# Attention with separate passes for the row maxima: the last head group's four chunks of queries taken in falling order

## The chip, the cores and the metric

One core of a Trainium2 chip. The metric is the device time of one execution in microseconds (us); lower is better.

## What is computed

One transformer block in float32 on x of shape (4, 2048, 256): a layer norm modulated by the condition, causal attention with 16 heads of 16 and rotary embedding, a gated residual, a second modulated layer norm, and a soft mixture of 8 experts. The change touches the attention alone:

```python
q = _rope((h @ Wq.T).reshape(B, S, H, hd).transpose(0, 2, 1, 3))
k = _rope((h @ Wk.T).reshape(B, S, H, hd).transpose(0, 2, 1, 3))
scores = jnp.einsum('bhqd,bhkd->bhqk', q, k) * scale
scores = jnp.where(causal, scores, jnp.finfo(scores.dtype).min)
attn = jax.nn.softmax(scores, axis=-1)
out = jnp.einsum('bhqk,bhkd->bhqd', attn, v)
```

## The kernel before

The four batches run one after the other. In each, the attention stage works through 16 **chunks** k = 0 to 15: four head groups g = k // 4 of 4 heads, and in each four chunks c = k % 4 of 512 queries. Chunk c sees 512(c + 1) keys, so it has 4c + 4 steps of 128 keys (`steps_of_chunk`). A step is cut into **units** of at most 512 columns of scores: 4 units in a full step, 4, 4, 2 and 1 in the four diagonal ones, so 11, 27, 43 and 59 units in the chunks c = 0 to 3, 140 in a head group and SU = 560 in a batch.

For each unit TensorE makes the scores of 128 keys by up to 512 queries in one of three PSUM banks (L634, on a diagonal also the mask, L638), and ScalarE takes the exponential (L913). Three units behind the end of a step, TensorE weighs the values with it (L654, 8 matmuls for 4 heads). After a chunk its result is copied by ScalarE (L902), turned (L664) and divided by its sums on VectorE (L1269, L1271).

The exponential needs the row's maximum beforehand. So there is a second stream, of **maxima**: TensorE makes the same scores with queries on the partitions (L560 to L574) in three other banks, and VectorE reduces each bank (`reduce_unit`, L1188). A chunk c has per head one "diag", one "odd" (two reductions), one "even" and 4c "full" maxima, 4(3 + 4c) = 12, 28, 44 or 60 in all. When a chunk's last one is reduced, VectorE combines them (`negmax`, L1205 to L1214, five small operations). Four maxima into the next chunk stands an entry "rows": TensorE turns the combined maxima (L560), VectorE copies them (L1184), and SP writes them by four DMAs into three extra rows of the queries (`load_bias`, L444). The first score unit of the chunk waits for them. With the 16 "rows" entries a batch has MU = 592 entries in the list MAXES.

The order on TensorE is written out ahead of time: ahead of score unit u it issues maxima until their number is `MAXES_BY[u]`, and VectorE follows the same list. `max_pace` makes it: a linear pace from lead = 60 at u = 0 to all 592 at u = `end`, which is 8 units ahead of the first unit of the last chunk, and at each chunk's first unit at least `ROWS_AT[k] + 8`, so that the chunk's maxima are on the way:

```python
    end = FIRST_UNIT[FIRST_STEP[NK - 1]] - behind
    least = {FIRST_UNIT[FIRST_STEP[k]]: min(MU, ROWS_AT[k] + behind) for k in range(NK)}
        out.append(max(out[-1] if out else 0, min(MU, lead + (MU - lead) * u // end), least.get(u, 0)))
```

The whole list is kept in order: a maximum that is called for early is not called for again, so behind a jump the pace is flat until the line has caught up. The first 41 maxima are made in the stage before (EARLY), 19 more beside the value projections. Keys and queries of a head group come by DMAs issued by ScalarE at fixed units (L916 to L922), and the output projection starts when all 16 chunks are done (L709).

Of the kernel before, what the change touches and what calls it, by code (L numbers as in the profile page):

```python
# [11 lines left out]
NC = 4  # L12
# [22 lines left out]
NG = H // HG  # L35
NK = NG * NC
VC = HD + 1


def steps_of_chunk(k):  # L40

    return 4 * (k % NC) + 4


STEPS = [(k, j) for k in range(NK) for j in range(steps_of_chunk(k))]
# [5 lines left out]
def diagonal(s):  # L51

    k, j = STEPS[s]
    return max(j - 4 * (k % NC), -1)

# [9 lines left out]

def max_units_of_chunk(k):

    c = k % NC  # L70
    for h in range(HG):
        yield k, h, "diag", 0, 0
        yield k, h, "odd", 0, 0
        yield k, h, "even", 0, 0
        for kc in range(c):
            for r in range(4):
                yield k, h, "full", r, kc
# [80 lines left out]
def adaln_block(nc, x, Wq, Wk, Wv, Wo, norm_gamma, slot_gamma, slot_embeds, w1, b1, w2, b2, cond, wmod,  # L158
                rope_cos, rope_sin, ident_in, mask_in, maskT_in, out):
    f32, bf16 = mybir.dt.float32, mybir.dt.bfloat16  # L160
    ALU, ACT, AX = mybir.AluOpType, mybir.ActivationFunctionType, mybir.AxisListType
# [8 lines left out]
    with ctx:  # L170
# [216 lines left out]
        def _(sp):  # L387
# [49 lines left out]
            for b in range(B):  # L437

                def load_bias(k):

                    g, c = divmod(k, NC)
                    sp.wait_ge(s_mxf, b * MU + (ROWS_AT[k] + 1 + NMX))
                    for h in range(HG):
                        sp.dma_start(qst[g % 2][KROWS:BROWS, h, c * CH:(c + 1) * CH],  # L444
                                     nrow[4 * PARTS * h:4 * PARTS * (h + 1), k % 3, :]).then_inc(s_bias[k % 3], 16)

                for k in range(NK):
                    load_bias(k)
                    if k == 0:
                        sp.wait_ge(s_o, b * NT) if b else None  # L450
                        sp.dma_start(modb[:, :, :].rearrange("p n d -> p (n d)"), mod_park[b:b + 1, :].to_broadcast([P, 4 * D])
                                     ).then_inc(s_modl, 16)
                sp.wait_ge(s_st, b * SU + (LAST_UNIT_OF_CHUNK[3 * NC - 1] + 1))
                sp.dma_start(xres, x[b].rearrange("(t p) d -> p t d", p=P)).then_inc(s_xr, 16)

                for c in range(NC):
                    sp.wait_ge(s_x1, b * 8 + 2 * c + 2)
                    sp.dma_start(x1_park[b, :, 1024 * c:1024 * c + 1024],
                                 xres[:, 4 * c:4 * c + 4, :].rearrange("p t d -> p (t d)")).then_inc(s_park, 16)

                def load_expert(e):
                    sp.dma_start(w1s[e % NR], w1[e].rearrange("(k p) h -> p k h", p=P)).then_inc(s_ew[e % NR], 16)
                    sp.dma_start(w2s[e % NR], w2[e].rearrange("(j p) d -> p j d", p=P)).then_inc(s_ew[e % NR], 16)
                for e in range(NR):
                    sp.wait_ge(s_sl, b * 16 + 4 * (e + 1))
                    load_expert(e)
                sp.wait_ge(s_sl, b * 16 + 16)
                sp.dma_start(b2b, b2.rearrange("(o e) d -> o e d", o=1).to_broadcast([P, E, D])).then_inc(s_b2, 16)
                if b + 1 < B:
                    load_x(b + 1)  # L470
                for e in range(NR, E):
                    sp.wait_ge(s_y, b * 8 + e - NR + 1)
                    load_expert(e)
                sp.wait_ge(s_eo, b * 8 + 8)
                sp.wait_ge(s_park, (b + 1) * 64)
                for c in range(NC):
                    sp.dma_start(x1[:, 4 * c:4 * c + 4, :].rearrange("p t d -> p (t d)"),
                                 x1_park[b, :, 1024 * c:1024 * c + 1024]).then_inc(s_x1r[c], 16)
                if b + 1 < B:
                    qkv_transfers(b + 1)  # L480
# [4 lines left out]
        def _(pe):  # L485
# [52 lines left out]
            def max_unit(b, m):  # L538

                k, h, kind, r, kc = MAXES[m]  # L540
                g, c = divmod(k, NC)
                bank = NST + m % NMX
                if m == FIRST_MAX[k]:
                    if g == 0:
                        if c == 0:
                            pe.wait_ge(s_rab, (b + 1) * QU)
                            pe.wait_ge(s_id, 1)
                        pe.wait_ge(s_ldf[c], (b + 1) * 112)
                    elif c == 0:
                        pe.wait_ge(s_ld[g % 2], (b * LOAD_USES[g % 2] + (g + 1) // 2) * 112)  # L550
                pe.wait_ge(s_mxf, b * MU + (m + 1))

                def qt(i):
                    return qst[g % 2][0:KROWS, h, i * P:(i + 1) * P]

                def kt(i, n):
                    return kst[g % 2][0:KROWS, h, i * P:(i + n) * P]
                if kind == "rows":
                    pe.wait_ge(s_nm, b * NK + (k + 1))
                    last = tr(ps[0:PARTS * HG * 4, bank, 0:P // 2].bitcast(bf16),  # L560
                              negp[:, :, :, :].rearrange("p h s t -> p (h s t)"), identb[:, :])
                elif kind == "diag":
                    mm(ps[:, bank, :], identb[:, :], maskb[:, :, :].rearrange("p r t -> p (r t)"),  # L563
                       start=True, stop=True)
                    for i in range(4):
                        last = mm(ps[:, bank, i * P:(i + 1) * P], qt(4 * c + i), kt(4 * c + i, 1),
                                  start=False, stop=True, skip_group_check=True)
                elif kind == "odd":
                    mm(ps[:, bank, 0:P], qt(4 * c + 1), kt(4 * c, 1), start=True, stop=True)
                    last = mm(ps[:, bank, P:4 * P], qt(4 * c + 3), kt(4 * c, 3), start=True, stop=True)  # L570
                elif kind == "even":
                    last = mm(ps[:, bank, 0:2 * P], qt(4 * c + 2), kt(4 * c, 2), start=True, stop=True)
                else:
                    last = mm(ps[:, bank, :], qt(4 * c + r), kt(4 * kc, 4), start=True, stop=True)  # L574
                last.then_inc(s_mx, 1)
# [29 lines left out]
            for b in range(B):  # L605
# [17 lines left out]
                def score_unit(u):  # L623

                    s, h0, n, w = UNITS[u]
                    k, j = STEPS[s]
                    g, c = divmod(k, NC)
                    if s == FIRST_STEP[k] and u == FIRST_UNIT[s]:
                        pe.wait_ge(s_bias[k % 3], (b * BIAS_USES[k % 3] + k // 3 + 1) * 64)
                    if u >= NST:  # L630
                        pe.wait_ge(s_ex, b * SU + (u + 1 - NST))
                    bank = ps[:, u % NST, :]
                    for i in range(n):
                        last = mm(bank[:, i * w:(i + 1) * w], kst[g % 2][0:BROWS, h0 + i, j * P:(j + 1) * P],  # L634
                                  qst[g % 2][0:BROWS, h0 + i, (c + 1) * CH - w:(c + 1) * CH],
                                  start=i == 0, stop=True, skip_group_check=True)
                    if diagonal(s) >= 0:
                        last = mm(bank[:, 0:n * w].rearrange("p (n w) -> p n w", n=n)[:, :, 0:P], identb[:, :],  # L638
                                  maskTb[:, 0:n, :], start=False, stop=True, skip_group_check=True)
                    last.then_inc(s_st, 1)  # L640

                def weigh(s):

                    k, j = STEPS[s]
                    g, c = divmod(k, NC)
                    w = CH - max(diagonal(s), 0) * P
                    if j == 0:
                        if k:
                            pe.wait_ge(s_ev, b * NK + k)
                        else:  # L650
                            pe.wait_ge(s_vone, b + 1)
                    pe.wait_ge(s_ex, b * SU + (LAST_UNIT[s] + 1))
                    for h in range(HG):
                        last = mm(ps[32 * h:32 * h + VC, 6, CH - w:CH], vall[:, j, HG * g + h, :], Eb[s % ESLOTS][:, h, 0:w],  # L654
                                  start=j == 0, stop=True, skip_group_check=True)
                    last.then_inc(s_pvq, 1)
# [449 lines left out]
        def _(dve):  # L1106
# [95 lines left out]
            def negmax(b, k):  # L1202

                dve.wait_ge(s_mxf, b * MU + (LAST_MAX[k] + 1 + NMX))
                V.tensor_reduce(negm[:, :, :], pm[:, k % 2, :, :, 0:2 + k % NC], AX.X, ALU.max, negate=True).then_inc(s_own_nm, 1)  # L1205
                at = 4 * (b * NK + k)
                dve.wait_ge(s_own_nm, at + 1)
                V.tensor_copy(negp[:, :, 0, :], negm[:, :, :]).then_inc(s_own_nm, 1)
# [50 lines left out]
            for b in range(B):  # L1259

                def gather(k):

                    g, c = divmod(k, NC)
                    if k == 0:
                        for i in range(QU - SETS_OF_BATCH[b], QU):
                            dve.wait_ge(s_pk[set_of(b, i)], set_parked(b, i))
# [190 lines left out]
```

## Time and profile before

| | us |
|---|---|
| median of 3 runs | 3474.62 (3473.63 to 3474.74) |
| the profiled execution | 3468.5, its span 3466.7 |
| TensorE busy | 3148.6 (91%) |
| VectorE busy | 2254.7 (65%) |
| ScalarE busy | 1848.3 (53%) |
| attention stage of one batch (first to last exponential) | 454.3 to 455.9, four times |

Times in the trace count from the start of the span. The k-th exponential of L913 in a batch is unit k, so the trace shows when each unit passes. Batch 1 runs its units from 1001.2 to 1456.7 us. A busy TensorE is not TensorE at its peak: the ends of its matmuls are modelled.

### The profile page before, as it was taken

The numbers are of one execution on the slowest core, as the hardware profiler recorded it, in microseconds if no ns is written. First come the engines' busy times: TensorE is split into PE (matmuls) and PEld (weight loads), VectorE is DVE, ScalarE is ACT, GpSimd is POOL, SyncE is SP. The second block draws the span as 40 slices with busy tenths as digits, with TensorE's granted clock in tenths as the row PEclk, the third lists the DMA queues.
The fourth block names the chain that finished last, engine by engine and source line by source line (L and its number), as shares of the span: only waits on it lengthen the run. The fifth ranks groups of instructions, "written<-read, shape, count | busy, mean of one in ns | idle before, by whom it ended". The sixth has DMA issues, their size and how long they took to land.

```text
span 3466.7 us, 45370 instructions
## 1 busy us (share of the span) xinstructions
PE 3148.6 (91%) x17663; PEld 1541.5 (44%) x17663; DVE 2254.7 (65%) x4309; ACT 1848.3 (53%) x3425; POOL 253.1 (7%) x139
## 2 busy tenths in 40 slices
PE   5799999898899999888989999988997999998999
PEld 2433332547553333353754333334575333333468
DVE  5878884662677788366367788836536877874632
ACT  2366667464236666645515666655641566665560
POOL 3100000110400000011030000000122000001100
PEclk9799999999999999999999999999999999999999
DMA  5222200015412120002542202010353221101042
GB/s 147 71 38 38 38 2 26 25 60 181 137 38 35 23 38 2 31 19 96 169 118 50 38 2 38 1 43 7 128 169 98 38 39 22 18 10 41 0 159 97
DMA packets 123694, 202.01 MB, mean 58 GB/s; under 512 B 10108, under 2 KB 107136, under 8 KB 120372
## 3 DMA queue, kind: packets, MB, share of 16 engines
q1 hardware_dynamic: 110960, 148.71, 13.3%
q10 hardware_dynamic: 12520, 50.40, 7.7%
q8 instruction: 140, 2.29, 0.3%
q14 instruction: 74, 0.61, 0.1%
HBM read 156.14 MB, written 42.16 MB: 57 GB/s over the span
## 4 chain that ended last, share of the span: by engine, by line
PE 71%; DVE 12%; ACT 7%; DMA 3%; issue 3%; POOL 2%; ACTq 1%; SPq 1%; DVEq 0%
PE ps L654 15%; PE ps L634 11%; PE ps L574 9%; PE ps L778 7%; PE ps L587 6%; DVE pm L1188 5%; PE ps L752 5%; ACT R L913 2%; PE ps L794 2%; DMA R<-in_L_ffn_w_dram 2%; PE ps L534 2%; PE ps L804 2%; PE ps L619 1%; PE ps L741 1%; PE ps L638 1%
## 5 line engine op out<-in xcount | busy, mean ns | idle before, releaser
L1188 DVE TENSOR_REDUCE pm<-ps 128x1 f32<-128x512 f32 (+4 forms) x2560 | 1395.2, 603 | 265.9 <-PE ps L574 190.1
L913 ACT ACTIVATE R<-ps 128x512 f32<-128x512 f32 (+1 forms) x2240 | 1190.5, 588 | 612.1 <-PE ps L634 418.7
L634 PE MATMUL ps<-R 99*128 99x512 bf16 (+3 forms) x2560 | 822.7, 354 | 26.8 <-ACT R L913 16.0
L654 PE MATMUL ps<-R 128*17 128x512 f32 (+3 forms) x5120 | 598.9, 541 | 24.5 <-ACT R L902 24.0
L574 PE MATMUL ps<-R 96*128 96x512 bf16 x1536 | 575.2, 385 | 24.7 <-DVE pm L1188 21.7
L634 PEld LDWEIGHTS ps<-R 99*128 99x128 bf16 x2560 | 238.4, 98 | 249.7 <-ACT R L913 139.6
L574 PEld LDWEIGHTS ps<-R 96*128 96x128 bf16 x1536 | 147.3, 97 | 453.1 <-DVE pm L1188 346.2
L778 PE MATMUL ps<-R 128*128 128x512 f32 x512 | 233.6, 615 | 12.2 <-ACT R L1005 12.2
L587 PE MATMUL ps<-R 128*128 128x257 f32 x1024 | 235.3, 385 | 4.1 <-ACT R L861 3.6
L752 PE MATMUL ps<-snT,R 128*128 128x512 f32 x512 | 229.8, 594 | 6.3 <-ACT R L951 6.3
L587 PEld LDWEIGHTS ps<-R 128*128 128x128 f32 x1024 | 196.5, 193 | 41.2 <-issue 12.1
L654 PEld LDWEIGHTS ps<-R 128*17 128x17 f32 x5120 | 86.1, 96 | 240.4 <-ACT R L913 117.9
L1096 POOL TENSOR_TENSOR R<-R,modb 128x1024 f32<-128x1024 f32 x16 | 37.6, 2349 | 2099.7 <-DVE R L1307 2099.7
L638 PE MATMUL ps<-maskTb,identb 128*128 128x128 bf16 (+2 forms) x704 | 172.6, 245 | 0.0
L778 PEld LDWEIGHTS ps<-R 128*128 128x128 f32 x512 | 100.6, 198 | 145.9 <-issue 124.8
L1269 DVE RECIPROCAL rden<-ps 128x16 f32<-128x16 f32 x64 | 16.0, 250 | 228.8 <-PE ps L664 228.8
L794 PE MATMUL ps<-R 128*128 128x128 f32 x1024 | 130.6, 291 | 27.9 <-DMA R<-in_L_ffn_w_dram 15.1
L563 PE MATMUL ps<-maskb,identb 128*128 128x512 bf16 x256 | 102.9, 402 | 56.9 <-DVE pm L1188 31.5
L1379 DVE TENSOR_TENSOR R<-ps,R 128x256 f32<-128x256 f32 x32 | 13.6, 425 | 204.7 <-PE ps L804 204.7
L794 PEld LDWEIGHTS ps<-R 128*128 128x128 f32 x1024 | 126.8, 205 | 37.4 <-DMA R<-in_L_ffn_w_dram 20.5
L894 ACT COPY R<-ps 128x512 f32<-128x512 f32 x32 | 18.7, 585 | 230.3 <-PE ps L619 230.3
L752 PEld LDWEIGHTS ps<-snT,R 128*128 128x128 f32 x512 | 93.0, 190 | 106.1 <-issue 95.6
(154 smaller groups left out, 3357.9 us busy)
## 6 DMA issues: line engine op xcount, KB each, us to landing
R<-in_L_ffn_w_dram SPq DMA_DIRECT2D x64, 1024.0 KB, 7.0
R<-q_parts ACTq DMA_DIRECT2D x12, 768.0 KB
R<-k_parts ACTq DMA_DIRECT2D x12, 768.0 KB
R<-in_L_attn_x_dram SPq DMA_DIRECT2D x16, 512.0 KB, 8.1
q_parts<-R SPq DMA_DIRECT2D x16, 512.0 KB, 3.8
k_parts<-R SPq DMA_DIRECT2D x16, 512.0 KB, 3.4
R<-in_L_attn_x_dram SPq DMA_DIRECT2D x4, 2048.0 KB, 8.4
x_park<-R SPq DMA_DIRECT2D x16, 512.0 KB, 2.6
```

Of the source, the lines that this page charges most:

```text
L534: last = mm(ps[:, 2 + 2 * qk + f, :], wqkT[:, k, 2 * qk + f, :], hT[:, k, c * CH:(c + 1) * CH], start=k == 0, stop=k == 1)
L563: mm(ps[:, bank, :], identb[:, :], maskb[:, :, :].rearrange("p r t -> p (r t)"), start=True, stop=True)
L574: last = mm(ps[:, bank, :], qt(4 * c + r), kt(4 * kc, 4), start=True, stop=True)
L587: last = mm(ps[:, 6 + n % 2, 0:D + 1], EcT[:, e, n * P:(n + 1) * P], eo[:, e, :], start=e == 0, stop=e == E - 1)
L634: last = mm(bank[:, i * w:(i + 1) * w], kst[g % 2][0:BROWS, h0 + i, j * P:(j + 1) * P], qst[g % 2][0:BROWS, h0 + i, (c + 1) * CH - w:(c + ...
L638: last = mm(bank[:, 0:n * w].rearrange("p (n w) -> p n w", n=n)[:, :, 0:P], identb[:, :], maskTb[:, 0:n, :], start=False, stop=True, skip_ ...
L654: last = mm(ps[32 * h:32 * h + VC, 6, CH - w:CH], vall[:, j, HG * g + h, :], Eb[s % ESLOTS][:, h, 0:w], start=j == 0, stop=True, skip_grou ...
L752: last = mm(ps[:, 4 + 2 * (n % 2) + mh, :], xnT[:, k, n * P:(n + 1) * P], snT[:, k, mh * 512:(mh + 1) * 512], start=k == 0, stop=k == 1)
L778: last = mm(ps[:, 2 * k + mh, :], xn[:, n, k * P:(k + 1) * P], L[:, n, mh * 512:(mh + 1) * 512], start=n == 0, stop=n == NT - 1)
L794: last = mm(ps[:, 2 * (e % 2) + j // 4, (j % 4) * P:(j % 4 + 1) * P], w1s[e % NR][:, k, j * P:(j + 1) * P], slotsT[:, k, e * P:(e + 1) * P ...
L913: A(Eb[s % ESLOTS][:, h0:h0 + n, 0:w], ps[:, u % NST, 0:n * w].rearrange("p (n w) -> p n w", n=n), ACT.Exp, scale=SCALE).then_inc(s_ex, 1)
L1188: mx = lambda o, i: V.tensor_reduce(o, i, AX.X, ALU.max)
```

## The change

`group_and_chunk(k)` takes the place of `divmod(k, NC)` and `k % NC` where a chunk's place is needed: in head group 3 the chunks k = 12 to 15 now stand for c = 3, 2, 1, 0 in place of 0, 1, 2, 3. All else follows from that: the order of units and maxima, the due times, and through FIRST_UNIT of chunk 15 the slope of the pace. The number of instructions on each engine is the same.

```diff
--- before.py
+++ after.py
@@ -37,9 +37,15 @@
 VC = HD + 1
 
 
+def group_and_chunk(k):
+
+    g, c = divmod(k, NC)
+    return g, NC - 1 - c if g == NG - 1 else c
+
+
 def steps_of_chunk(k):
 
-    return 4 * (k % NC) + 4
+    return 4 * group_and_chunk(k)[1] + 4
 
 
 STEPS = [(k, j) for k in range(NK) for j in range(steps_of_chunk(k))]
@@ -51,7 +57,7 @@
 def diagonal(s):
 
     k, j = STEPS[s]
-    return max(j - 4 * (k % NC), -1)
+    return max(j - 4 * group_and_chunk(k)[1], -1)
 
 
 
@@ -67,7 +73,7 @@
 
 def max_units_of_chunk(k):
 
-    c = k % NC
+    c = group_and_chunk(k)[1]
     for h in range(HG):
         yield k, h, "diag", 0, 0
         yield k, h, "odd", 0, 0
@@ -438,7 +444,7 @@
 
                 def load_bias(k):
 
-                    g, c = divmod(k, NC)
+                    g, c = group_and_chunk(k)
                     sp.wait_ge(s_mxf, b * MU + (ROWS_AT[k] + 1 + NMX))
                     for h in range(HG):
                         sp.dma_start(qst[g % 2][KROWS:BROWS, h, c * CH:(c + 1) * CH],
@@ -538,7 +544,7 @@
             def max_unit(b, m):
 
                 k, h, kind, r, kc = MAXES[m]
-                g, c = divmod(k, NC)
+                g, c = group_and_chunk(k)
                 bank = NST + m % NMX
                 if m == FIRST_MAX[k]:
                     if g == 0:
@@ -546,7 +552,7 @@
                             pe.wait_ge(s_rab, (b + 1) * QU)
                             pe.wait_ge(s_id, 1)
                         pe.wait_ge(s_ldf[c], (b + 1) * 112)
-                    elif c == 0:
+                    elif k % NC == 0:
                         pe.wait_ge(s_ld[g % 2], (b * LOAD_USES[g % 2] + (g + 1) // 2) * 112)
                 pe.wait_ge(s_mxf, b * MU + (m + 1))
 
@@ -624,7 +630,7 @@
 
                     s, h0, n, w = UNITS[u]
                     k, j = STEPS[s]
-                    g, c = divmod(k, NC)
+                    g, c = group_and_chunk(k)
                     if s == FIRST_STEP[k] and u == FIRST_UNIT[s]:
                         pe.wait_ge(s_bias[k % 3], (b * BIAS_USES[k % 3] + k // 3 + 1) * 64)
                     if u >= NST:
@@ -642,7 +648,7 @@
                 def weigh(s):
 
                     k, j = STEPS[s]
-                    g, c = divmod(k, NC)
+                    g, c = group_and_chunk(k)
                     w = CH - max(diagonal(s), 0) * P
                     if j == 0:
                         if k:
@@ -1202,7 +1208,7 @@
             def negmax(b, k):
 
                 dve.wait_ge(s_mxf, b * MU + (LAST_MAX[k] + 1 + NMX))
-                V.tensor_reduce(negm[:, :, :], pm[:, k % 2, :, :, 0:2 + k % NC], AX.X, ALU.max, negate=True).then_inc(s_own_nm, 1)
+                V.tensor_reduce(negm[:, :, :], pm[:, k % 2, :, :, 0:2 + group_and_chunk(k)[1]], AX.X, ALU.max, negate=True).then_inc(s_own_nm, 1)
                 at = 4 * (b * NK + k)
                 dve.wait_ge(s_own_nm, at + 1)
                 V.tensor_copy(negp[:, :, 0, :], negm[:, :, :]).then_inc(s_own_nm, 1)
@@ -1260,7 +1266,7 @@
 
                 def gather(k):
 
-                    g, c = divmod(k, NC)
+                    g, c = group_and_chunk(k)
                     if k == 0:
                         for i in range(QU - SETS_OF_BATCH[b], QU):
                             dve.wait_ge(s_pk[set_of(b, i)], set_parked(b, i))
```

## Rows read from the trace of the kernel before

**Rows 1.** The page: span, busy time of the engines, costliest groups of the attention stage

```profile
span 3466.7 us, 45370 instructions
...
PE 3148.6 (91%) x17663; PEld 1541.5 (44%) x17663; DVE 2254.7 (65%) x4309; ACT 1848.3 (53%) x3425; POOL 253.1 (7%) x139
...
L1188 DVE TENSOR_REDUCE pm<-ps 128x1 f32<-128x512 f32 (+4 forms) x2560 | 1395.2, 603 | 265.9 <-PE ps L574 190.1
L913 ACT ACTIVATE R<-ps 128x512 f32<-128x512 f32 (+1 forms) x2240 | 1190.5, 588 | 612.1 <-PE ps L634 418.7
L634 PE MATMUL ps<-R 99*128 99x512 bf16 (+3 forms) x2560 | 822.7, 354 | 26.8 <-ACT R L913 16.0
L654 PE MATMUL ps<-R 128*17 128x512 f32 (+3 forms) x5120 | 598.9, 541 | 24.5 <-ACT R L902 24.0
L574 PE MATMUL ps<-R 96*128 96x512 bf16 x1536 | 575.2, 385 | 24.7 <-DVE pm L1188 21.7
```

**Rows 2.** Windows over the attention stage of batch 1 and of batch 0; columns as named

```profile
core 0: us, PE busy (x) PEld busy (x) DVE busy (x) ACT busy (x) POOL busy (x), PEclk, DMA share, GB/s
1001.00:1457.00 456.00, 435.51 (x2939) 153.79 (x2940) 336.59 (x687) 302.80 (x576) 0.00 (x0) 0.98 0.15 27
150.00:606.00 456.00, 434.29 (x2936) 153.58 (x2935) 336.68 (x687) 302.21 (x575) 0.00 (x0) 0.98 0.15 27
```

**Rows 3.** Windows of batch 1: full pace with maxima, and the tail without maxima

```profile
1315.00:1355.00 40.00, 39.77 (x267) 14.46 (x267) 33.46 (x70) 27.48 (x52) 0.00 (x0) 1.00 0.01 2
1426.00:1450.00 24.00, 21.68 (x128) 4.87 (x124) 0.68 (x2) 20.75 (x41) 0.00 (x0) 1.00 0.07 23
```

**Rows 4.** Windows, exponentials (L913) alone: the same two stretches

```profile
core 0: us, ACT busy (x), PEclk, DMA share, GB/s
1315.00:1355.00 40.00, 27.48 (x52) 1.00 0.01 2
1426.00:1450.00 24.00, 20.75 (x41) 1.00 0.07 23
```

**Rows 5.** Groups kept apart by form: the reductions of the maxima (mean ns of one)

```profile
L1188 DVE TENSOR_REDUCE pm<-ps 128x1 f32<-128x512 f32 x1536 | 972.9, 683 | 192.1 <-PE ps L574 190.1
L1188 DVE TENSOR_REDUCE pm<-ps 128x4 f32<-128x512 f32 x256 | 175.5, 686 | 30.2 <-PE ps L566 27.8
L1188 DVE TENSOR_REDUCE pm<-ps 128x1 f32<-128x384 f32 x256 | 139.7, 546 | 0.0
L1188 DVE TENSOR_REDUCE pm<-ps 128x1 f32<-128x256 f32 x256 | 106.1, 415 | 22.9 <-PE ps L572 21.0
...
L1188 DVE TENSOR_REDUCE pm<-ps 128x1 f32<-128x128 f32 x256 | 72.1, 282 | 20.6 <-PE ps L570 20.3
```

**Rows 6.** Timeline of DVE in the burst ahead of unit 81, batch 1; start, length, what

```profile
1065.15 0.69 DVE L1188 TENSOR_REDUCE pm<-ps 128x1 f32<-128x512 f32 x1 [0.59 <-PE ps L574]
1065.87 0.23 DVE L1205 TENSOR_REDUCE negm<-pm 128x16 f32<-128x80 f32 x1
...
1066.77 0.17 DVE L1214 TENSOR_TENSOR negp<-negr,negp 128x16 bf16<-128x16 f32 x1
1066.86 2.42 DVE L1188 TENSOR_REDUCE pm<-ps 128x4 f32<-128x512 f32 x5
1069.20 0.21 DVE L1184 COPY nrow<-ps 48x128 bf16<-48x128 bf16 x1
1069.36 1.09 DVE L1188 TENSOR_REDUCE pm<-ps 128x1 f32<-128x128 f32 x3
1070.62 3.17 DVE L1188 TENSOR_REDUCE pm<-ps 128x4 f32<-128x512 f32 x7 [0.17 <-PE ps L566]
```

**Rows 7.** Timeline of ACT at the three bursts of batch 1

```profile
1062.90 1.81 ACT L913 ACTIVATE R<-ps 128x512 f32<-128x512 f32 x3
1074.18 1.08 ACT L913 ACTIVATE R<-ps 128x512 f32<-128x512 f32 x2 [9.47 <-PE ps L634]
...
1184.06 1.32 ACT L913 ACTIVATE R<-ps 128x512 f32<-128x512 f32 x2
1191.97 1.08 ACT L913 ACTIVATE R<-ps 128x512 f32<-128x512 f32 x2 [6.60 <-PE ps L634]
...
1306.60 0.60 ACT L913 ACTIVATE R<-ps 128x512 f32<-128x512 f32 x1 [0.17 <-PE ps L638]
1311.04 1.09 ACT L913 ACTIVATE R<-ps 128x512 f32<-128x512 f32 x2 [3.84 <-PE ps L634]
```

**Rows 8.** Windows: the bursts ahead of units 81 and 221, and maxima alone in the prologue

```profile
1064.70:1074.00 9.30, 6.95 (x39) 3.20 (x35) 8.12 (x22) 0.01 (x1) 0.00 (x0) 0.66 0.01 1
1185.00:1191.90 6.90, 4.80 (x35) 1.83 (x27) 6.07 (x16) 0.38 (x1) 0.00 (x0) 0.91 0.01 2
110.00:120.00 10.00, 9.33 (x28) 2.94 (x28) 10.00 (x23) 0.00 (x0) 0.00 (x0) 0.50 0.23 69
```

**Rows 9.** One line (L634), all of it: the score matmuls, ns min/median/max

```profile
L634 PE MATMUL ps<-R x2560: 216/379/635, 149.3 to 3152.3; 99*128 99x512 bf16 x139, 99*128 99x384 bf16 x20, 99*128 99x128 bf16 x19, 99*128 99x256 bf16 x19
```

**Rows 10.** Windows, exponentials (L913) alone: 9 us behind the burst at unit 221, batches 1 and 2

```profile
1191.90:1200.90 9.00, 4.97 (x9) 0.50 0.01 2
2042.60:2051.60 9.00, 7.03 (x14) 1.00 0.00 0
```

**Rows 11.** Timeline of SP in the burst at unit 81: the rows of maxima to the queries

```profile
1069.43 2.92 SPq L444 DMA_DIRECT2D R<-nrow  x4
```

**Rows 12.** Timeline: end of the attention stage of batch 1

```profile
1455.73 1.57 ACT L913 ACTIVATE R<-ps 128x512 f32<-128x512 f32 x3
...
1456.43 1.49 PE L654 MATMUL ps<-R 128*17 128x384 f32 x24
...
1457.99 0.58 ACT L902 COPY R<-ps 128x512 f32<-128x512 f32 x1 [0.68 <-PE ps L654]
...
1459.61 0.42 DVE L1271 TENSOR_TENSOR R<-ps,rden 128x256 f32<-128x256 f32 x1
...
1460.09 1.09 PE L705 MATMUL ps<-ident,R 128*128 128x128 f32 x8 [0.81 <-DVE R L1271]
```

## The prediction

> **What bounds the kernel now.** I began with the page: TensorE is busy for 91% of the span, VectorE 65%, ScalarE 53%, and three of the five costliest groups are TensorE's matmuls of the attention stage [rows 1]. The windows over that stage show it four times alike, 456 us, TensorE busy for 434 to 436 of them [rows 2]. So attention takes 4 x 455 = 1820 of the 3467 us, and there TensorE is the engine to watch.
>
> The change leaves the work alone and alters its order, so I need prices for the three ways in which the plan mixes the two streams:
> - **Mixed**, at the full pace of (592 - 60) / 493 = 1.079 maxima per score unit. In 40 us 52 exponentials pass, 0.769 us per unit [rows 4], with TensorE busy 39.77 of 40 us and VectorE 33.46 [rows 3]. TensorE bounds it.
> - **Flat**, score units without maxima, as in the tail of a batch: 41 exponentials in 24 us, 0.585 us per unit [rows 4]; TensorE is busy 21.68 us, ScalarE 20.75, VectorE nearly idle [rows 3]. The pair and its three banks bound it.
> - **Burst**, maxima without score units, where a due time lifts the plan. Before batch 1's unit 81 there are 13, before 221 there are 10, before 361 there are 7. ScalarE idles there for 9.47, 6.60 and 3.84 us [rows 7], and VectorE is at work almost throughout [rows 6, 8]. A burst runs at VectorE's price: 683 ns for a full one, 686 a diagonal one, 282 + 546 an odd one, 415 an even one [rows 5], 0.21 for "rows" and 1.1 for the five operations of a chunk's end [rows 6]. For the 13: 4 x 0.686 + 4 x 0.828 + 3 x 0.415 + 0.683 + 0.21 + 1.1 = 9.3 us; exponential to exponential was 1074.18 - 1064.11 = 10.07 [rows 7] (the three from 1062.90 on end at 1064.71, and the last began 0.60 earlier), less about 0.54 for the score unit itself, 9.5. The price holds.
>
> **What the change does to the plan.** I worked out MAXES_BY from the formula for both orders.
>
> The slope's end moves from unit 493 to 560 - 11 - 8 = 541, as chunk 15 now has 11 units. The pace falls from 1.079 to 532 / 541 = 0.983. The due times don't fall with it. At unit 420 (chunk 12) the maxima of a chunk with c = 3 are now wanted, 60 and not 12: due are ROWS_AT + 8 = 516, the pace has brought 472 at unit 419, and 44 come at once; before, only 468 were due and the pace was at 513. At 479 chunk 13 wants 561 where 530 are there, 31; at 522 chunk 14 wants 590, 18 more. In head groups 0 to 2, whose order is unchanged, the slower pace makes the old jumps larger and opens new ones: 21 at unit 81 (13 before), 12 at 178, 31 at 221 (10), 4 at 291, 23 at 318, 41 at 361 (7). Behind every jump the plan is flat until the line has caught up.
>
> Per batch: maxima in bursts 30 before, 225 after (+195). Units in flat stretches 90 before (66 of them the tail from 494 on), 239 after (+149).
>
> **The sum.** Let p be what a unit costs TensorE-bound, q what a maximum adds to it; p + 1.079 q = 0.769. Units and maxima are the same in number, so only what leaves the mix changes the time:
> change = 149 (0.585 - p) + (burst time after - before) - 195 q.
> - Burst time after: 144 full, 24 diagonal, 26 odd, 23 even and 8 "rows" make 98.4 + 16.5 + 21.5 + 9.5 + 1.7 = 147.6 us, and 7 chunk ends 7.7: 155.3. Before, by the same prices, 18.9 + 1.1 = 20.0. Difference 135.3 us.
> - q: no row shows it alone. The shortest score matmul, as wide as a full maximum, is 216 ns [rows 9]; I take 0.216, so p = 0.536. If the flat stretch were TensorE-bound too, q = (0.769 - 0.585) / 1.079 = 0.170 at least; the mean duration of a full maximum, with its pipeline, is 0.385 at most [rows 1]. The sum hardly depends on it: 0.170 gives 0 + 135.3 - 33.2 = 102.1; 0.216 gives 7.3 + 135.3 - 42.1 = 100.5; 0.385 gives 149 x 0.231 = 34.4, so 34.4 + 135.3 - 75.1 = 94.6. I take **100.5 us per batch**.
> - TensorE's clock. In a burst TensorE waits for VectorE (4.80 us busy of 6.90), and in the first two bursts of batch 1 the granted clock falls to half (means 0.66 and 0.91) [rows 8]. It stays there into the flat stretch: in the 9 us behind unit 221 batch 1 passes 9 exponentials at 0.50, batch 2, where it did not fall, 14 at 1.00 [rows 10]. That is 1.0 us against 0.64 per unit, 3.2 us. After the change eight bursts per batch have 12 maxima or more. At 3 us each that is 24; before, one full and one partial such loss, about 4. I add **20 us per batch**. Bounds: nothing (the clock comes back inside a long burst) and 43.
> - The burst itself costs no more at half clock: in the prologue VectorE is busy 10.0 of 10.0 us with maxima at 0.50 [rows 8].
> - "Rows": SP issues four DMAs in 2.92 us from 1069.43 [rows 11], and the exponential comes at 1074.18 [rows 7], 0.4 us behind the last maximum (1070.62 + 3.17). The eight entries from "rows" on cover the DMAs, as they will in every burst. Nothing; if SP were late, 1 us for each of eight.
> - The order itself: head group 3's keys come before chunk 8 begins and serve all four chunks, and the output projection waits for all of them. The last chunk ends in the same four diagonal steps, so the drain of some 4 us [rows 12] stays. Nothing; at most 1 us either way.
>
> 120.5 x 4 = 482 us. The profiled execution, 3468.5 us, would become 3950; the median lies 6.1 above it, so **3956**, taken as 3955.
>
> The rule for the clock is also in the Trainium skill (TensorE: Matmul & The Clock Gate, "Part 1: The HAM clock gate"): half rate is the array's default state, and activity releases it. It speaks against every long burst; without it the sum would be 3877, with it 3956.
>
> **The rivals.**
> - **The clock comes back only with the mix** (7%). All 239 flat units then run at 1.0 us, 0.415 more each, 99 us in place of 24: 195 per batch, 3474.6 + 782 = 4257. For it: 9 us at 0.50 behind a burst [rows 10]. Against it: TensorE is busy for most of a flat stretch, and the batch 1 tail runs at 1.00 throughout [rows 3].
> - **No more is lost to the clock than before** (15%): 3474.6 + 4 x 100.5 = 3877. For it: behind unit 221 of batch 2 nothing was lost [rows 10].
> - **Faster** (2%): the due times at 420, 479 and 522 don't decide, and what counts is the shorter tail. The flat stretches would shrink from 90 to 24 + 18 units with bursts as before: -48 x 0.049 = -2.4 us per batch, 3465; with q = 0.385, -48 x 0.231 = -11, 3430. It needs the pace to lie above 516 at unit 420; it is at 473. Above that point nothing bursts in group 3.
> - **No effect** (1%): the jumps are absorbed, as ScalarE has slack. It would need more than three score banks between the engines, since ScalarE stopped for 9.47 us at 13 maxima [rows 7].
>
> The forecast itself has 75%.
>
> **How the numbers follow.** Low end: 94 per batch and no clock loss, 3474.6 + 376 = 3851. High end: 102 per batch and a clock loss of 43 more than before, 3474.6 + 580 = 4055. With the rival at 4257 left out and misses of the price of a burst allowed for (0.1 us per burst maximum would be 78 us), about 2 in 10 lie outside 3850 to 4060. 0.2% is what a measurement of this kernel can tell from no change, 7 us; every case but two is far beyond it: slower 0.97, same 0.01, faster 0.02.
>
> **What would show it.** Attention per batch 575 us and not 455, and the other stages the same. VectorE's and ScalarE's busy time unchanged, TensorE's share near 80%. Idle of ScalarE ahead of unit 420 of some 29 us, 28 at 361, 20 at 221 and 479, each released by a score matmul, with VectorE busy through it. Flat stretches behind them at 0.59 us per unit, 1.0 for the first few where the clock is at half. Mixed stretches at 0.536 + 0.983 x 0.216 = 0.75. Wrong would be: bursts that run faster than 0.6 us per maximum, or an idle ScalarE that falls short of these lengths; a second wait on the "rows" DMAs; half clock through whole flat stretches.

## The result, and the profile after

The changed kernel takes 3950.4 us (median; 3948.2 to 3956.2) against 3474.1 us: a ratio of 1.137, 95% interval 1.1355 to 1.1384. The forecast was 3955. It was right in size and in mechanism, but several of its terms were off and cancelled.

From the page of the changed kernel: span, busy time, two slice rows, and the groups that answer to [rows 1]. The line numbers are 6 higher than before.

```profile
span 3954.4 us, 45207 instructions
...
PE 3438.9 (87%) x17500; PEld 1588.8 (40%) x17663; DVE 2254.4 (57%) x4309; ACT 1831.7 (46%) x3425; POOL 253.3 (6%) x139
...
PEclk9888878899998887899999887789999988788999
DMA  5320100115422010011532110000242212000033
...
L1194 DVE TENSOR_REDUCE pm<-ps 128x1 f32<-128x512 f32 (+4 forms) x2560 | 1388.7, 603 | 668.2 <-PE ps L580 350.9
L919 ACT ACTIVATE R<-ps 128x512 f32<-128x512 f32 (+1 forms) x2240 | 1173.5, 588 | 1113.0 <-PE ps L640 943.5
L640 PE MATMUL ps<-R 99*128 99x512 bf16 (+3 forms) x2560 | 832.0, 380 | 139.1 <-DMA R<-nrow 96.6
L580 PE MATMUL ps<-R 96*128 96x512 bf16 x1536 | 643.5, 438 | 81.3 <-DVE pm L1194 76.5
```

VectorE's and ScalarE's busy times have hardly moved. What grew is idle time: VectorE ahead of its reductions from 265.9 to 668.2 us, ScalarE ahead of its exponentials from 612.1 to 1113.0 us, 500 us more. Each engine waits for TensorE while TensorE works through the entries of the other stream. TensorE's own busy time rose by 290 us without an added instruction, and its mean granted clock fell from 0.965 to 0.883: it ran at half clock for longer. And one releaser is new among the large ones: `DMA R<-nrow`, the rows of maxima, 96.6 us.

Windows of batch 1 of the changed kernel: the whole attention stage, the burst ahead of unit 420, and two stretches of the flat plan behind it. They answer to [rows 2, 3, 8].

```profile
core 0: us, PE busy (x) PEld busy (x) DVE busy (x) ACT busy (x) POOL busy (x), PEclk, DMA share, GB/s
1121.00:1697.00 576.00, 505.93 (x2898) 164.29 (x2936) 335.88 (x687) 298.26 (x575) 0.00 (x0) 0.84 0.12 21
1541.00:1567.00 26.00, 21.79 (x57) 5.53 (x56) 25.83 (x52) 0.00 (x0) 0.00 (x0) 0.59 0.00 1
1568.00:1576.40 8.40, 8.04 (x37) 2.25 (x37) 0.41 (x2) 4.84 (x9) 0.00 (x0) 0.50 0.01 2
1576.40:1583.60 7.20, 6.56 (x37) 1.22 (x35) 0.27 (x1) 6.22 (x13) 0.00 (x0) 0.99 0.00 1
```

The stage takes 576 us where it took 456. In the burst VectorE is busy 25.83 of 26 us and ScalarE does nothing. Behind it the clock is at 0.50 for 8.4 us, then at 0.99.

Timeline of ScalarE in the same batch, at unit 151, then ahead of units 361 and 420, answering to [rows 7]:

```profile
1257.45 0.60 ACT L919 ACTIVATE R<-ps 128x512 f32<-128x512 f32 x1 [7.58 <-PE ps L640]
...
1473.29 0.60 ACT L919 ACTIVATE R<-ps 128x512 f32<-128x512 f32 x1 [0.35 <-PE ps L644]
1499.56 1.09 ACT L919 ACTIVATE R<-ps 128x512 f32<-128x512 f32 x2 [25.67 <-PE ps L640]
...
1568.01 1.09 ACT L919 ACTIVATE R<-ps 128x512 f32<-128x512 f32 x2 [27.46 <-PE ps L640]
```

The two long stops stand where the plan has its jumps of 41 and 44. The first one, at unit 151, stands where the plan has no jump at all.

### The profile page after: what moved, and what is told of

The parts are those of the page before. It is cut to its first block, busy times and chain, and to the rows that moved or that the text cites. A ratio compares the mean times of both kernels' runs of the same rounds, so it can differ in the third digit from the quotient of the medians.

```text
span 3954.4 us, 45207 instructions
## 1 busy us (share of the span) xinstructions
PE 3438.9 (87%) x17500; PEld 1588.8 (40%) x17663; DVE 2254.4 (57%) x4309; ACT 1831.7 (46%) x3425; POOL 253.3 (6%) x139
## 3 DMA queue, kind: packets, MB, share of 16 engines
q1 hardware_dynamic: 110960, 148.71, 11.8%
## 4 chain that ended last, share of the span: by engine, by line
PE 61%; DVE 18%; ACT 7%; DMA 7%; issue 3%; SPq 2%; POOL 1%; ACTq 1%; DVEq 0%
PE ps L660 14%; PE ps L640 12%; DVE pm L1194 11%; PE ps L784 5%; PE ps L593 5%; PE ps L580 5%; DMA R<-nrow 4%; PE ps L758 4%; ACT R L919 3%; PE ps L800 2%; DMA R<-in_L_ffn_w_dram 2%; PE ps L540 2%; PE ps L810 2%; SPq L450 2%; PE ps L625 1%
## 5 line engine op out<-in xcount | busy, mean ns | idle before, releaser
L1194 DVE TENSOR_REDUCE pm<-ps 128x1 f32<-128x512 f32 (+4 forms) x2560 | 1388.7, 603 | 668.2 <-PE ps L580 350.9
L919 ACT ACTIVATE R<-ps 128x512 f32<-128x512 f32 (+1 forms) x2240 | 1173.5, 588 | 1113.0 <-PE ps L640 943.5
L640 PE MATMUL ps<-R 99*128 99x512 bf16 (+3 forms) x2560 | 832.0, 380 | 139.1 <-DMA R<-nrow 96.6
L580 PE MATMUL ps<-R 96*128 96x512 bf16 x1536 | 643.5, 438 | 81.3 <-DVE pm L1194 76.5
L660 PE MATMUL ps<-R 128*17 128x512 f32 (+3 forms) x5120 | 637.0, 574 | 27.6 <-ACT R L908 21.3
L572 PE MATMUL ps<-R 96*128 96x128 bf16 x1024 | 119.7, 249 | 44.6 <-DVE maskTb L1250 14.9
L644 PE MATMUL ps<-maskTb,identb 128*128 128x128 bf16 (+2 forms) x665 | 156.8, 236 | 0.0
```

What stands on the lines that cost most here:

```text
L919: A(Eb[s % ESLOTS][:, h0:h0 + n, 0:w], ps[:, u % NST, 0:n * w].rearrange("p (n w) -> p n w", n=n), ACT.Exp, scale=SCALE).then_inc(s_ex, 1)
L1194: mx = lambda o, i: V.tensor_reduce(o, i, AX.X, ALU.max)
```

## The account of one batch

The start times of the 560 exponentials of batch 1, sorted by what the plan does ahead of each unit, give this account (us; the change as forecast stands beside it):

| | before | after | change | forecast |
|---|---|---|---|---|
| units with a burst ahead (3; 9) | 21.7 | 162.1 | +140.4 | 135.3 + 6 x 0.536 = +138.5 |
| flat units (90; 239) | 59.6 | 169.5 | +109.9 | 149 x 0.585 + 20 = +107.2 |
| mixed units (466; 311) | 374.3 | 244.2 | -130.1 | -155 x 0.536 - 195 x 0.216 = -125.2 |
| sum | 455.6 | 575.8 | +120.2 | +120.5 |

The first row counts the gap from the exponential before the burst to the one behind it. In the first row are 10.7 us, and in the third 7.4 us, of a wait that the forecast had at nothing. The gap at unit 291 lasts 14.3 us for 4 maxima worth 2.7 by the forecast's prices and 0.8 for the unit itself; that at unit 151 lasts 8.2 us where 0.8 is usual in the mix. Without these waits the bursts cost 129.7 and not 138.5, and the mix saves 137.5 and not 125.2.

## Experiments

All ratios are against the kernel before, on the same chip.

**1. Order and slope apart.** The falling order with the old slope:

```diff
+++ changed kernel, max_pace
-    end = FIRST_UNIT[FIRST_STEP[NK - 1]] - behind
+    end = 493
```

> The falling order kept, the slope of the pace put back by hand (end = 493 in place of 541). Theory (the lost time comes from the flatter slope alone): 34 maxima in bursts and 93 flat units per batch, as before but for one jump of 4 at unit 420, so 1 us per batch: 3474 + 4 = 3478 us, 3465 to 3490. Rival (the order itself costs, since the chunk with most keys now comes first in its group and wants 60 maxima at once): the three bursts of group 3, 93 of the 195 added burst maxima, stay, and some 40% of the loss with them: about 3665 us.

Measured: 3485.5 us, ratio 1.0027 (1.0015 to 1.004). And the rising order with the new slope:

```diff
+++ kernel before, max_pace
-    end = FIRST_UNIT[FIRST_STEP[NK - 1]] - behind
+    end = 541
```

> The rising order of before, with the flatter slope alone (end = 541). Theory (slope alone): 221 maxima in bursts, 234 flat units, eight bursts over 12: by the same prices 118 us per batch, 3948 us, 3920 to 3975. Rival (order and slope each bring their part): bursts of groups 0 to 2 only, 132 maxima, 102 more than before, about 62 us per batch: 3722 us.

Measured: 3959.7 us, ratio 1.139 (1.137 to 1.1405). So the slope alone brings the whole loss, in either order, and the order alone 10 us of 476. The rising kernel now has its own long stop ahead of its last chunk, 41 maxima at unit 501. Timeline of ScalarE in it:

```profile
1633.35 2.31 ACT L913 ACTIVATE R<-ps 128x384 f32<-128x384 f32 x4 [1.04 <-PE ps L638]
1666.31 1.08 ACT L913 ACTIVATE R<-ps 128x512 f32<-128x512 f32 x2 [30.65 <-PE ps L634]
```

The diff does not touch the line that did it. `end` hangs on the length of the last chunk: 59 units at the end kept the pace steep, 11 units don't. The steep line was behind the due time at 3 of the 15 later chunks; the flat one is behind at 9 of them, and what is missing is then made up at once.

The order by itself costs 10 us where 4 were expected. In the trace of the steep falling kernel chunk 11, with the jump of 4 behind it, takes 1.6 to 3.5 us longer per batch than before. In two of the four batches the clock also falls to half behind unit 361, where the plan is still that of before, so not all of the 10 us need be the order's. The steep falling kernel there, then the kernel before at the same place in batch 1:

```profile
1315.90:1322.70 6.80, 6.60 (x32) 1.24 (x32) 2.04 (x4) 4.24 (x8) 0.00 (x0) 0.50 0.00 0
1310.20:1317.00 6.80, 5.95 (x48) 2.21 (x47) 3.50 (x12) 4.78 (x9) 0.00 (x0) 1.00 0.01 2
```

**2. The clock behind a burst.** Needless matmuls behind each maximum of the eight long bursts, into the bank of the output transposes. The added wait lets TensorE write there only when VectorE has read what an earlier chunk left in it:

```diff
+                    burst = u and MAXES_BY[u] - MAXES_BY[u - 1] > 10
+                    if burst:
+                        pe.wait_ge(s_on, b * NK + STEPS[UNITS[u][0]][0] - 1)
                     while m < MAXES_BY[u]:
                         max_unit(b, m)
                         m += 1
+                        if burst:
+                            for w in (512, 256):
+                                mm(ps[:, 7, 0:w], zerosb[:, :], maskb[:, :, :].rearrange("p r t -> p (r t)")[:, 0:w],
+                                   start=True, stop=True)
```

> The changed kernel, with two needless matmuls of 512 and 256 columns into the bank of the output transposes behind each maximum of the eight long bursts, so that TensorE is busy in them. They add work and nothing to the output. Theory (3.0 us behind six bursts and 1.3 behind two are the clock at half, and it falls since TensorE waits in the burst): the granted clock stays at 1.00 from burst to flat, the bursts keep their length (0.22 + 0.32 us of TensorE under 0.62 of VectorE), and 4 x 20.6 = 82 us go: 3868 us, 3850 to 3895. Rival (the slow units behind a burst are the start of the pipeline and three banks, whatever the clock): no change or slower, 3950 to 3990.

Measured: 3849.8 us, ratio 1.108 (1.106 to 1.110), so 101 us less than the changed kernel for more work. Below are windows of the burst ahead of batch 1's unit 420 and of the 5.4 us behind it, then ScalarE's stop there in the timeline.

```profile
1494.00:1520.00 26.00, 24.85 (x144) 12.37 (x145) 25.52 (x51) 0.00 (x0) 0.00 (x0) 1.00 0.01 1
1521.10:1526.50 5.40, 4.57 (x37) 1.48 (x36) 0.14 (x1) 4.77 (x9) 0.00 (x0) 1.00 0.00 0
```

```profile
1521.19 2.30 ACT L926 ACTIVATE R<-ps 128x512 f32<-128x512 f32 x4 [27.34 <-PE ps L640]
```

The clock is at 1.00 in both, where it was 0.59 and 0.50. The stop has its old length, 27.34 us for 27.46, so the burst goes at VectorE's pace at either clock level. The first 8 units behind each of the eight bursts take 5.44 or 5.45 us in this batch, where the changed kernel takes 8.43 (six times) and 6.73 or 6.74 (twice). The half clock, and not the start of the pipeline, is what makes these units dear. That is 20.6 us per batch, 82 in all, of the 101 gained. By the start times of all four batches, the flat units as a whole take 89 us less than in the changed kernel, the units with a burst 11 us less (0.1 to 0.5 us for each gap), the mixed ones 3. The time at half clock within the four attention stages falls from 734 to 82 us; before it was 68.

The Trainium skill (TensorE: Matmul & The Clock Gate, "Part 1: The HAM clock gate") says that activity releases the half rate, and this pair of runs agrees: the same burst with TensorE kept at work shows 1.00, against 0.59.

**3. The two stops without a burst.** Timelines of the changed kernel, batch 1: ScalarE issues the queries and keys of group 3 behind unit 279; SP issues chunk 9's rows of maxima; then come the last three exponentials ahead of the stop, and that of unit 291.

```profile
1380.99 1.26 ACTq L386 DMA_DIRECT2D R<-q_parts  x3
1382.28 1.81 ACTq L388 DMA_DIRECT2D R<-k_parts  x4
...
1388.74 2.92 SPq L450 DMA_DIRECT2D R<-nrow  x4
...
1389.81 1.81 ACT L919 ACTIVATE R<-ps 128x512 f32<-128x512 f32 x3 [0.56 <-PE ps L644]
1405.28 1.09 ACT L919 ACTIVATE R<-ps 128x512 f32<-128x512 f32 x2 [13.67 <-PE ps L640]
```

The rows go out at 1388.7, and the exponential that needs them starts at 1405.3. In the burst of the kernel before, they were issued at 1069.43 [rows 11] and used at 1074.18 [rows 7]. The DMA queues of the changed kernel show what is under way in between. Queue q10 carries ScalarE's seven transfers, 3.1 MB in all, and q1 the four of SP, 3 KB each. The first line is the window 1388 to 1397 us, in which q1 has no packet; the other two are 1397 to 1403.5 us:

```profile
q10 hardware_dynamic: 135, 1.49, 100.4%
q10 hardware_dynamic: 79, 0.66, 53.5%
q1 hardware_dynamic: 60, 0.01, 1.6%
```

The last packet of the rows starts 14.5 us behind the issue, where it was 3.7 us in the burst at unit 81 before. At unit 151 it is 18.0 us, though SP issues the rows there 1.0 us ahead of ScalarE's first transfer. I moved the large transfers:

```diff
-                        if u == LAST_UNIT_OF_CHUNK[NC * (g - 1) - 1]:
+                        if u == LAST_UNIT_OF_CHUNK[NC * (g - 1) - 1] + 13:
                             load_group(act, g, slice(0, T), s_ld[g % 2])
```

> The changed kernel, with the keys and queries of head groups 2 and 3 fetched 13 units later (behind the first units of chunks 5 and 9, not ahead of them). In the changed kernel's trace ScalarE waits 14.3 us ahead of unit 291, where only 4 maxima stand, and 8.2 us ahead of unit 151, where there is no burst; the rows of maxima were issued just behind the 1.5 MB of keys there. Theory (the small transfers queue behind the large ones): both waits go, 10.7 + 7.4 = 18 us per batch, 3950 - 72 = 3878 us, 3860 to 3900. Rival (SP or the maxima are late by themselves there): no change, 3950.

Measured: 3862.1 us, ratio 1.111 (1.109 to 1.113): 88 us less than the changed kernel. The gap from unit 290 to 291 falls from 14.3 to 2.5 us, that from 150 to 151 from 8.2 to 1.3. SP and ScalarE at unit 291 of that run:

```profile
1359.11 2.92 SPq L450 DMA_DIRECT2D R<-nrow  x4
1363.87 0.60 ACT L919 ACTIVATE R<-ps 128x512 f32<-128x512 f32 x1 [1.89 <-PE ps L640]
```

So the large transfers had held up the small ones. By this the two waits are 11.8 and 6.9 us per batch, 75 in all. In the kernel before, the steeper pace had sent chunk 5's rows off at 1107.3 us in batch 1, and the large transfers followed at 1117.4.

That is 16 us more than the 72 expected. I put them down to ScalarE's own issue, and tested that in the kernel before, with the same edit:

> The kernel before, with the keys of head groups 2 and 3 fetched 13 units later and nothing else. Theory (late keys brought 88 us in the changed kernel: 72 by the two waits for rows of maxima, which the kernel before does not have, and 16 by ScalarE's issue of the DMAs at the chunk's end, which it has): 3475 - 16 = 3459 us. Rival (all of the 88 us are waits for rows of maxima): 3475.

Measured: 3495.2 us, ratio 1.0053 (1.0033 to 1.0073). Both expectations fail: it is 20 us slower. ScalarE in batch 1 of that run:

```profile
1140.34 0.60 ACT L913 ACTIVATE R<-ps 128x512 f32<-128x512 f32 x1 [0.22 <-PE ps L634]
1140.35 1.41 ACTq L380 DMA_DIRECT2D R<-q_parts  x3
1141.79 1.79 ACTq L382 DMA_DIRECT2D R<-k_parts  x4
1143.63 1.57 ACT L913 ACTIVATE R<-ps 128x512 f32<-128x512 f32 x3 [2.69 <-issue]
```

The seven issues stop ScalarE for 2.69 us in the midst of the mix, where TensorE soon waits for it. The stops at units 140 and 280 did shorten, from 3.2 to 1.6 and from 3.4 to 1.4 us in batch 1, but chunk 5 then took 27.2 us in place of 23.7. The clock has a part in that: behind each of the eight such stops of this run it is at half for 3.4 us, and at none of these places in the kernel before. How much of the price that is was not set apart. Behind unit 151 of batch 1, first this run, then the kernel before:

```profile
1146.10:1149.50 3.40, 3.40 (x16) 1.37 (x9) 0.69 (x1) 1.17 (x3) 0.00 (x0) 0.51 0.97 142
1135.40:1138.80 3.40, 3.40 (x23) 1.15 (x22) 3.37 (x7) 2.17 (x4) 0.00 (x0) 1.00 0.47 87
```

The start times of the changed kernel with late keys place its gain in batch 1, 20.6 us: 18.7 are the two waits, 4.1 the shorter stops at units 140 and 280, and 1.7 the units behind the burst at 318, which pass sooner at full clock. The moved issues take some 3 us of that back in chunks 4, 5 and 8. Why they take 8.6 us back in the kernel before (chunks 4, 5, 8 and 9) is open.

**4. The pace levelled.** If a maximum costs more in a burst than in the mix, a plan without bursts must beat both kernels. Between the due times it takes the smallest slopes that meet them all:

```diff
+    points = [(0, values_by(7))] + [(FIRST_UNIT[FIRST_STEP[k]], min(MU, ROWS_AT[k] + behind)) for k in range(1, NK)]
+    out = [0] * SU
+    at = points[0]
+    while at[1] < MU:
+        to = max((p for p in points if p[0] > at[0] and p[1] > at[1]),
+                 key=lambda p: ((p[1] - at[1]) / (p[0] - at[0]), p[0]))
+        for u in range(at[0], to[0] + 1):
+            out[u] = at[1] - (-(to[1] - at[1]) * (u - at[0]) // (to[0] - at[0]))
+        at = to
+    for u in range(at[0], SU):
+        out[u] = MU
```

> The falling order, with the pace levelled: between the due times it takes the smallest slopes that meet them all (1.22, 1.06, 1.03, 0.76, 0.67 maxima per unit), so there is no burst at all, 35 flat units. Theory (a burst maximum costs 0.65 us where one in the mix costs 0.22 to 0.3, and a flat unit saves almost nothing): 20 us per batch less than before, 3394 us, 3375 to 3430. Rival (the mix is bound at 0.77 us per unit by VectorE's pace, so that 1.22 per unit stalls as a burst does): 3474 or more.

> The rising order with the same levelling of the pace: slopes 1.22, 1.06, 0.98, all maxima made by unit 501, no burst, 59 flat units at the end. Theory: 19 us per batch less than before, 3398 us, 3380 to 3435, so within 0.5% of the falling order with the levelled pace: the order is then worth the spread of 24 flat units, under 2 us per batch. Rival (the falling order is worth something by itself once the plan is level, since its tail is shorter): the falling one faster by over 20 us.

Measured: falling 3391.6 us, ratio 0.9756 (0.974 to 0.977); rising 3432.2 us, 0.988 (0.986 to 0.990). The falling one came out as expected and is the fastest kernel of this study. Its attention stage, and in it a stretch with the steepest pace and one with the gentlest:

```profile
981.00:1416.00 435.00, 423.61 (x2932) 151.37 (x2934) 337.54 (x687) 303.92 (x574) 0.00 (x0) 1.00 0.15 28
1010.00:1045.00 35.00, 33.85 (x224) 11.52 (x223) 31.46 (x61) 22.80 (x43) 0.00 (x0) 1.00 0.56 92
1365.00:1405.00 40.00, 38.60 (x277) 13.60 (x275) 19.55 (x49) 32.09 (x62) 0.00 (x0) 1.00 0.01 3
```

435 us at a clock of 1.00, TensorE 97% busy over the stage, VectorE at 90% where the pace is steep. The rising one lies at the upper end of its range, and its rival held: the order is worth 40 us here, not under 8. Part of it is a wait ahead of unit 501, where the last due time leaves nothing to cover the rows of maxima. Waits of the rising levelled kernel around it (us in total, times, longest):

```profile
ACT R L918 <- PE ps L639: 5.1, 3, 3.8
PEld ps L639 <- DMA R<-nrow: 3.8, 1, 3.8
PE ps L639 <- DMA R<-nrow: 3.1, 1, 3.1
```

So I had all maxima made by unit 493, with one more point:

```diff
+    points.append((493, MU))
```

> The rising order with the levelled pace and all maxima due by unit 493 in place of 501, as the pace of before had it. Theory (of the 9 us per batch that the rising levelled kernel takes above the falling one, 3.4 are the wait for the last rows of maxima at unit 501, whose DMAs nothing covers): 3432 - 4 x 3 = 3420 us, 3412 to 3428; the rest of the gap to 3392 stays. Rival (all of the gap is that wait): 3395. Second rival (the wait moves to 493 with its cost): 3432.

Measured: 3406.5 us, ratio 0.980 (0.9785 to 0.982). It gained 26 us, twice the forecast. The forecast counted the wait alone, and the clock goes with it. In and behind unit 501's wait the rising levelled kernel is at half clock for 6.8 us, and with the early end it is not. Windows of batch 1, first without and then with the early end:

```profile
1395.60:1402.40 6.80, 4.00 (x22) 0.82 (x22) 0.00 (x0) 1.99 (x4) 0.00 (x0) 0.50 0.58 181
1384.50:1391.30 6.80, 5.83 (x51) 1.85 (x44) 0.00 (x0) 5.70 (x13) 0.00 (x0) 1.00 0.59 187
```

15 us remain between the orders. The rising order makes its last maxima within the 81 units of three short chunks and leaves 59 flat units, or 66 with the early end; the falling order spreads them up to unit 536. In the traces head group 3 takes 98.1 us of batch 1 in the rising order with the early end and 94.9 in the falling one, so most of the 4 us per batch lie there. That these units are the cause was not tested.

Last, the levelled falling plan with the late keys:

> The falling order with the levelled pace and the keys of head groups 2 and 3 fetched 13 units later. Theory (issuing the seven DMAs costs ScalarE 3.1 us while it holds up the exponentials at units 140 and 280, where it waits 3.2 to 4.5 us; behind the first units of a chunk this is hidden): 2 x 2.2 us per batch, 3392 - 18 = 3374 us. Rival (the stop at 140 and 280 is the end of the chunk, and comes with any order of issue): 3392, or above it if the later keys collide with other rows of maxima.

Measured: 3410.5 us, ratio 0.981 (0.979 to 0.983), 19 us slower than without them. The edit helped only where rows of maxima were held up; in a level plan none are, and the stop in the mix is all that it brings, as in the rising kernel (20 us). Here too the clock has a part: the time at half clock within the four attention stages rises from 3 to 34 us.

## Why the prediction was right, and where it was not

- **The plan.** Bursts of 21, 12, 31, 4, 23, 41, 44, 31 and 18 maxima were worked out from the formula, and ScalarE stops there. That the slope's end moves with the last chunk was the decisive reading, and experiment 1 confirms it. The prediction gave due times and slope the credit together; the runs give it to the slope: with the steep one the due time at 420 asks for 4 more maxima and not 44.
- **The price of a burst.** Summing the mean durations of the reductions gave 152.5 us for the eight bursts other than 291; they take 143.5 (gaps less 0.54 for the unit). At unit 420 the sum says 29.2 + 1.1 = 30.3 us, and the gap, score unit included, is 28.06. Reductions back to back start closer than they last. In this burst 12 full ones, recorded at 0.678 us each, fill 7.3 us with no idle time, where 12 x 0.678 would be 8.1; their starts lie 0.60 us apart. The reductions that run between 1544.4 and 1550.9 us:

```profile
L1194 DVE TENSOR_REDUCE pm<-ps 128x1 f32<-128x512 f32 x12 | 7.3, 678 | 0.0
```

The forecast's test of the price, the burst at unit 81, came out right by luck. The overlap is there as well (the diagonal one that starts at 1066.86 lasts 0.686 us, and the next starts 0.60 behind it), but VectorE was busy for only 8.12 of 9.30 us [rows 8], and its idle time made up for what the sum had too much.
- **What the mix gives back.** -137.5 us and not -125.2. The forecast's bounds (94.6 to 102.1 in the sum) took one p for every unit. At these prices the 466 mixed units of before should take 358 us; they take 374. The units at a chunk's start are dearer than the rest: in batch 1 of the kernel before, mixed units among the first 12 of a chunk take 0.87 us, the others 0.77. The 168 units that leave the mixed class took 6.5 us more than their price, and with a burst ahead of them they now pass in the flat class. Another 6.0 us come from 298 units that are mixed in both kernels and became cheaper by more than q for each maximum that left them. Why these did is open; no run set either part apart.
- **The 0.216.** It was read off the wrong row. The shortest score matmul is not as wide as a full maximum: it is the form of 128 columns, and one of 512 columns is recorded at 388 ns in the mean. The value is right all the same, since the 512-column matmuls of the maxima (L574) start 0.217 us apart at the median in the trace before. That was luck, and by the forecast's own bounds the sum hardly hung on it. From the kernel before:

```profile
L634 PE MATMUL ps<-R 99*128 99x512 bf16 x1792 | 666.2, 388 | 24.8 <-ACT R L913 14.0 <-DMA R<-nrow 8.9
L634 PE MATMUL ps<-R 99*128 99x128 bf16 x256 | 25.1, 220 | 0.0
```

- **The rows of maxima.** "Nothing; if SP were late, 1 us for each of eight" was the step that failed: two waits, 7.4 and 10.7 us, 72 us over four batches. I had looked at bursts only. The slower pace also makes the rows later where there is no burst, and twice a batch that put them among 3.1 MB of queries and keys (the expectation of late_keys names 1.5 MB, the keys alone). A second wait on the "rows" DMAs was among the prediction's own signs of being wrong, and it came.
- **The clock.** 20 us per batch were added. Experiment 2 finds 3.0 us behind six bursts and 1.3 behind two, 20.6 us. The kernel before had 4.3 of it in batch 1 (6.74 and 8.43 us for 8 units where 5.44 is full clock), so the net is 16.3 and not 20. (The upper bound of 43 stands in the prediction without a working.) The flat units made up for it: their row is 2.7 us above the forecast, so apart from the clock they cost 6.4 us more than 149 x 0.585. With the clock held up they take 0.618 us each (147.8 us for 239). Of the rivals, "no more is lost to the clock" falls, and so does "the clock comes back only with the mix": it is back 8.4 us into the flat stretch.
- **Faster, or no effect.** Neither: the due times did bite, and of the 28.06 us at unit 420 ScalarE idles for 27.46, so the three score banks absorb next to nothing.
- **The signs.** Stage and stops came as named (576 us for 575; 27.5, 25.7 and about 20 us). TensorE's share did not: near 80% was named, and it is 87% of the span and 88% of the stage, as its matmuls last longer at half clock (those of the maxima 438 ns in the mean, 385 before).

Over four batches the errors were -35 us (bursts), -49 (mix), +72 (rows) and +11 (flat units, clock). They cancel to about a microsecond by luck; each alone would have stayed inside the range.

## What to carry to other kernels

When a plan is written out ahead of time, print it before and after an edit, all of it: here a formula hung on the length of the last item, and reordering one quarter of the work changed the pace of the other three. Two streams that share an engine should be mixed as evenly as their due times allow; a burst costs the slower partner's price and idles the other, and the flat stretch that follows does not give it back. When durations from a profile are added up, compare the sum with the starts of a row of them. And when something small is made later, ask which large transfer it now stands behind.

## What was not expected of the hardware

Consecutive reductions of 512 columns from PSUM start 0.60 us apart though each is recorded at 0.68. Two needless matmuls per maximum made the kernel 101 us faster, by keeping the granted clock at full through the bursts. And moving two sets of seven DMA issues on ScalarE by 13 units cost 5 us per batch where nothing waited for the data, though it shortened two other stops: behind each such stop in the midst of the mix (2.7 us at chunk 5 of batch 1) the granted clock was at half for 3.4 us.
